# Attention: the products for the row maxima issued in bundles at every odd step of a unit, none at even steps

## What is computed

```python
Q = _multilora(x, ids, Wq, Aq, Bq)   # the same for K and V
Q, K = (_rope(Q), _rope(K))          # 16 heads of 16
scores = jnp.einsum('bhqd,bhkd->bhqk', Q, K) / jnp.sqrt(16)
scores = jnp.where(causal, scores, -jnp.inf)
attn = jax.nn.softmax(scores, axis=-1)
out = jnp.einsum('bhqk,bhkd->bhqd', attn, V)
return _multilora(out, ids, Wo, Ao, Bo)
```

## Time and profile before

| | us |
|---|---|
| median of 3 runs | 2032.51 |
| lowest and highest | 2030.67, 2043.24 |
| profiled execution, its own time | 2058.66 |
| span of its profile | 2057.0 |
| mean granted TensorE clock | 0.906 |

### The profile page before, as it was taken

The page is one execution under the profiler, slowest core; times in us unless marked ns, Lnnn a source line. Parts: engine busy times, 40 slices in busy tenths (PEclk is TensorE's granted clock), DMA queues, the critical chain, the costliest instruction groups (busy, mean ns, idle before and its releaser), DMA issues. The chain is left out here.

```text
span 2057.0 us, 32460 instructions
## 1 busy us (share of the span) xinstructions
PE 1803.7 (88%) x10701; PEld 1199.7 (58%) x10701; DVE 1290.4 (63%) x3148; ACT 877.0 (43%) x1799; POOL 724.4 (35%) x873
## 2 busy tenths in 40 slices
PE   5579989999989895499999968999899947999998
PEld 4133444444434333488888844848485736888886
DVE  4477677777676703755555528777777766555554
ACT  2146665665665743122222216474747451222221
POOL 2326355464463421123222213434343312232221
PEclk9668999999897957699999979999999978999999
DMA  5623353442544715267676642020202044676764
GB/s 157 211 80 114 113 150 108 127 129 93 152 132 143 224 53 193 94 241 258 240 257 243 240 143 83 1 103 1 103 1 103 1 186 184 239 260 238 259 244 173
DMA packets 103472, 312.39 MB, mean 152 GB/s; under 512 B 23304, under 2 KB 54796, under 8 KB 93200
## 3 DMA queue, kind: packets, MB, share of 16 engines
q1 hardware_dynamic: 84304, 257.06, 35.6%
q0 software_dynamic: 15936, 50.35, 8.1%
q10 hardware_dynamic: 3072, 2.90, 0.5%
HBM read 245.12 MB, written 53.87 MB: 145 GB/s over the span
## 5 line engine op out<-in xcount | busy, mean ns | idle before, releaser
L774 ACT ACTIVATE a_probs<-a_ps_e 128x512 f32<-128x512 f32 (+3 forms) x768 | 336.0, 491 | 183.3 <-PE a_ps_e L949 180.1
L511 DVE CUSTOM_DVE_ANT_0 a_ps_m<-a_ps_m,a_causal 128x512 f32<-128x512 f32 (+3 forms) x512 | 238.3, 517 | 84.1 <-PE a_ps_m L936 83.3
L1460 ACT CAST hidden_high<-g_ps_h 128x512 fp32r<-128x512 f32 x140 | 75.2, 590 | 398.8 <-PE g_ps_h L1605 398.8
L515 DVE TENSOR_REDUCE a_peak<-a_ps_m 128x1 f32<-128x512 f32 x256 | 164.1, 683 | 101.2 <-PE a_ps_m L936 99.9
L966 PE MATMUL a_ps_a<-a_probs,a_vals 128*32 128x256 f32 (+2 forms) x2560 | 216.8, 415 | 1.2 <-ACT a_probs L774 0.6
L949 PE MATMUL a_ps_e<-a_q_st,a_k_st 64*128 64x512 f32 (+3 forms) x768 | 189.6, 487 | 29.3 <-ACT a_probs L774 19.8
L653 POOL TENSOR_SCALAR_AFFINE_SELECT a_probs<-a_probs 128x256 f32<-128x256 f32 x256 | 104.5, 410 | 288.8 <-ACT a_probs L774 287.4
L936 PE MATMUL a_ps_m<-a_k_st,a_q_st 64*128 64x512 f32 (+3 forms) x768 | 157.0, 408 | 49.5 <-DMA a_k_st<-a_scr_k 23.0
L949 PEld LDWEIGHTS a_ps_e<-a_q_st,a_k_st 64*128 64x128 f32 x768 | 80.1, 204 | 199.2 <-ACT a_probs L774 137.7
L111 POOL TENSOR_TENSOR g_xe_rs<-g_xe_ve,table 128x1 f32<-128x1 f32 x70 | 39.4, 563 | 441.3 <-DVE g_xe_ve L1301 441.3
L1593 PE MATMUL g_ps_y<-g_w_d,hidden_high 128*128 128x512 f32 x560 | 144.2, 400 | 5.9 <-DVE x_res L1337 5.9
(11 more groups left out here) (316 smaller groups left out, 3907.3 us busy)
## 6 DMA issues: line engine op xcount, KB each, us to landing
g_w_d<-down_rows SPq DMA_DIRECT2D x70, 2048.0 KB, 7.8
a_q_st<-a_scr_q POOLq DMA_DIRECT2D x32, 512.0 KB, 4.4
a_k_st<-a_scr_k POOLq DMA_DIRECT2D x32, 512.0 KB, 5.5
m_spread_acs<-m_acs_rows SPq DMA_DIRECT2D x8, 2048.0 KB, 10.0
a_scr_q<-a_high SPq DMA_DIRECT2D x34, 256.0 KB
a_scr_k<-a_high SPq DMA_DIRECT2D x32, 256.0 KB
a_swapped<-a_raw SPq DMA_DIRECT2D x64, 128.0 KB, 2.0
g_x_rows<-x_res SPq DMA_DIRECT2D x8, 1024.0 KB, 12.5
```

Of the source, the lines that this page charges most:

```text
L511: nc.vector.tensor_tensor_reduce(ps_m[:, bank, 0:w], ps_m[:, bank, 0:w], causal[:, 512 - w:], 1.0, MASKED, ALU.add, ALU.max, peak[:, p % 2 ...
L515: nc.vector.tensor_reduce(peak[:, p % 2, r, i, c:c + 1], ps_m[:, bank, 0:w], AX, ALU.max).then_inc(chunk_max, 1)
L774: nc.scalar.activation(probs[:, N % RING, r, q0:], ps_e[:, (2 * N + r) % HEAD_BANKS, q0:], ACT.Exp, scale=DH ** -0.5).then_inc(exp_done, 1)
```

## The change

Two lines are added behind the table of cuts:

```diff
     CUTS = [cut(1 + LEAD)] + [cut(1 + U + LEAD + core_at[n]) for U in range(UNITS) for n in range(CORE)]
+    for N in range(0, UNITS * CORE, 2):
+        CUTS[N + 1] = CUTS[N]
```

## The result

| | before | changed |
|---|---|---|
| median of 4 runs, us | 2035.53 | 2091.16 |
| lowest and highest, us | 2030.67, 2043.24 | 2084.92, 2093.06 |
| profiled execution: span, us | 2057.0 | 2083.2 |
| first shifted product to unit 15, us | 605.6 | 657.7 |
| unit 15, first to last step, us | 49.3 | 30.4 |

The ratio is 1.0251, with a 95% interval of 1.0220 to 1.0282: 2.5% slower. The forecast was 2092.5 us.

A forecast was written before the change was run, and what follows sets the result against it. Attention steps were taken as bound by the 1.24 us exponential gate or TensorE's work and bank waits, not VectorE's total. 53 us of waits and gates plus 7 for the clock on 2032.5 gave 2092.5 us, range 2055 to 2130.

The forecast's parts named there:

- An empty step pays its gate: Full-width steps of attention: never shorter than 1.24 us even empty, since the next shifted product waits for the first exponential.
- Step 11: 2.55 us, a stand of 1.3: Three-pair step of each unit: third pair waits for the first's banks; with empty step 10, 3.79 us against 2.84, +0.95.
- Unit 6: Attention unit with a low-rank piece: +0.95, +0.85, +0.6 and +1.1 us over its steps, 3.5 us in all.
- The transpose of step 19: Unit 6: fifth user of four banks, waits 1.53 us for the step's own first product; step 19 takes 2.2 us.
- The projection of step 5: Projection piece behind three pairs: starts 2.04 us into the step where it was 1.11, +0.93 us.
- Output pieces: Units 4, 8, 12, odd steps 15 to 21: start 1.27 (step 17) and 2.17 us (step 19) in; 5.9 us a unit.
- The rule of the banks: Odd steps: with four banks, a further user waits until VectorE has read the step's own earlier product, plus some 0.12 us.
- The sum of 53 us: All units of attention: new waits and gates added up, 53 us; 26 from below.
- The clock: 7 us: Attention: new TensorE stands put some 21 us more at the lower clock, 0.33 us each; 7 us, range 0 to 35.
- rival (a): The clock falls at step 11 or step 5 in most units: 53 + 35 us and a few more, 2125; chance 0.22.
- rival (c): Faster: banks always free at odd steps, so the 36.4 us of L936 waits go; about 20 us lower, 2012; chance 0.04.
- (b): Bank waits hide in the even steps' idle time, or VectorE starts sooner: about +12 us, 2044; chance 0.10.

The follow-up runs named there:

- only3: Kernel before with only the pairs of steps 4, 10 and 14 moved on one step, so only the three-pair steps are new; ratio 1.0171 to the kernel before.
- cap2: The change without its three-pair steps: pairs of steps 4, 10 and 14 stay where they were; ratio 1.0060 to the kernel before.
- even: Mirror image of the change: pairs of each odd step issued one step earlier, odd steps left empty; 2091.6 us, ratio 1.0280 to the kernel before.
- half_after: The changed kernel with each maximum taken over the first half of its chunk only; 2039.1 us, ratio 1.0000 to the kernel before.
- pieces_even: The changed kernel with most pieces and the transposes of the maxima moved on to even, empty steps; 2105.6 us, ratio 1.0342 to the kernel before.

## Why the prediction was right, point by point

**An empty step pays its gate.** Right. Step 8 of unit 6 took 1.23 us, and step 10, now empty, 1.25 us where it took 1.57 with two pairs. Step 12 took 1.13 from product to product (409.69 to 410.82), but its first product had started 0.24 us after its weight load; from load to load it is 1.36.

**Step 11: 2.55 us, a stand of 1.3.** Right: 2.52 and 1.29 us. only3 shows that the three-pair steps are two thirds of the loss.

**Unit 6.** From the begin of step 10 to unit 7 the kernel before took 18.84 us; with the change it took 21.31 (405.92 to 427.23), +2.5, and I had +2.4 (0.95, 0.85 and 0.6). The transpose of step 19 starts 1.76 us into the step, 0.2 later than I counted. The projection of step 5 starts 1.07 us later, for my 0.93. The whole unit grew by 2.9 us for my 3.5, with the first steps of the kernel before at the lower clock; unit 11, at 1.00 in both, grew by 3.6 for my 3.2.

**Output pieces.** They start 1.20 and 2.05 us into their steps for my 1.27 and 2.17. The rule of the banks gives the start of these two within 0.12 us, that of the projection (2.18 for 2.04) within 0.14 and that of the transpose within 0.23. But units 4, 8 and 12 grew by 4.4, 5.2 and 3.1 us, and I had 5.9 for each: mis-sized. Units 1, 5, 9 and 13 grew by 0.0, 3.0, 2.0 and 1.5 for my 2.5, unit 0 by 5.2 for my 3. These lengths hold the clock's swings. TensorE's recorded idle time holds less of them: it grew by 3.0, 3.4 and 2.8 us in units 4, 8 and 12, by 2.1, 2.2, 1.6 and 3.0 in units 1, 5, 9 and 13, and by 5.5 in unit 0.

**The sum of 53 us.** Attention grew by 52 to 54 us, with the clock's part in it. Waits and gates alone are then 42 to 46. The recorded idle time, another way to the same number, grew by 46 us against the profile of before and by 41 against that of the unchanged kernel. So the sum is some 7 to 12 us too high. By the idle time 8.5 us of it lie in units 4, 8 and 12 (9.2 for 17.7), and unit 0 gives 2.5 back; the four units 1, 5, 9 and 13 have 8.9 for 10, and the six like unit 6 have 20.5 for 20.1. A slip of 0.3 us is in the sum itself: unit 2 has no low-rank piece and was counted as if it had.

**The clock: 7 us.** The time at the lower level grew by 24 us against the profile of before and by 38 against that of the unchanged kernel; I had taken 21. At 0.25 to 0.3 us each this is 6 to 11 us. TensorE's recorded busy time grew by 6.4 and 12.6 us against the two profiles, 0.26 and 0.33 us for each: my price of 0.33 stands at the upper end.

The upper end of the term, 35 us, was not reached with the change, but rival (a) has a part that is true. In the stretch up to unit 15 the trace's record of the granted clock shows it fall 2 times in steps 10 to 13 before, 3 times in the unchanged kernel's profile and 2 with cap2; it shows 8 such falls with the change, 13 with only3 and 11 with even, all with three pairs in step 10 or 11. In half_after, where the third pair's products stood 11.0 us in all for 19.4, there is none. Each count is from one profile, but they agree: where a third pair stood long, a fall of the clock followed in half of the units and more. I had kept the term near its low end because only a stand of 1.5 us was seen ahead of a fall; with the change and with even, falls came behind third pairs that stood 1.3 and 0.9 us. even and pieces_even, with 217 and 195 us at the lower level, show how near the upper end was.

The Trainium skill's account of short pauses that make the clock swing (page "TensorE: Matmul & The Clock Gate", section "A second HAM failure mode: psum-queue depth-cycling") agrees with these falls in part: the sum of the pauses doesn't decide, since only3 has more waits than even and 149 us at the lower level for 217.

**Where the argument failed though the number held.** For rival (a) I took unit 15, at clock 0.51, as a sign that empty steps bring the clock down. The unchanged kernel shows the same unit at 1.00, and its steps are not empty: `keep_warm` issues a product in each, and TensorE was recorded busy for 51.53 of 52.17 us. I read the 36.4 and 151.6 us of the earlier trace rows as waits of products and of loads; each is the sum of both, and the products' own are 8.7 and 19.8 us. No term of the sum was worked out from these two, but rival (c) was: its 20 us of gain were taken from a wait that is counted twice. And I put the changed kernel's profiled execution at 2119 us, adding 60 to the profile of before; it was 2084.9, 34 less. Of these, 19 us were the chance of this unit in the profile of before, 8 are what the forecast has too much in attention (60 for 52), and 7 lie outside attention. The median, on which the forecast was set, was the better base, though the 2032.5 us of three runs were 3 below the 2035.5 of four. That forecast and median came to lie 1.3 us apart is in part luck: a growth 4.4 us too high stood on a base 3.0 too low.

**Rivals (b) and (c).** Both are out. The waits on a step's own products are not hidden (only3). The waits of the maxima loads and products fall only from 28 and 9 to 24 and 6 us where no step has three pairs (cap2), and even so nothing is gained.

**What stays open:** why the clock falls in one unit and not in its like. Unit 3 grew by 8.0 and unit 14 by 7.8 us, where their idle time grew by 2.6 and 1.7; unit 10 didn't grow at all, with 4.5 us more of idle time and a clock of 1.00 for 0.86. With the mirror image, even, unit 6 alone of units 2, 3, 6, 7, 10 and 11 kept the clock up in steps 10 to 12. No run here shows what makes the difference.

## What to carry to other kernels

Where every step has a floor set by another engine, work that fits under the floor is free in each step once; moving it together gives little back in the emptied steps and pays in the full ones. Count, for a ring of n buffers, how many users a step issues: the (n+1)th waits for a reader that has only just been fed, and the price is product, read and semaphore in full (here 2.2 us for the third pair). Where a view adds the waits of loads and of products, look at each alone before a wait is taken for time that can be won. Before adding a change to a profiled time, ask whether the profiled execution is like the median; one stretch of chance clock was worth 19 us here.

## What the runs showed of the hardware that I had not expected

Work of no use made attention shorter in the profiles of three kernels: a filler pair in idle parts of steps took 44 to 59 us off the time at the lower clock level (1.2 GHz) and 13 to 15 us off attention; in a second profile of one of them it was 17 to 31 and 7 to 8. The medians gave 0.5 to 0.8%, near the scatter of an unchanged kernel. In kernels with three pairs of products in step 10 or 11 the granted clock fell in steps 10 to 13 of 8 to 13 of the 15 units, where no filler was added and VectorE read whole chunks. Without three pairs in a step it was 2 or 3 units, and with them and halved reads none. The same program took 49 us from the first to the last step of its last unit at a granted clock of 0.51 in one execution and 30 at 1.00 in another. A kernel unchanged measured 1.0057 against itself, with an interval that leaves out 1.
